# Selector products of k and q over 64 rows in a chunked delta-rule recurrence, both leaf parities issued in turn

## The reference

```python
def step(S, t):
    q_t, k_t, v_t, a_t, b_t = t
    y = jnp.einsum('bhvk,bhk->bhv', S, k_t)
    err = y - v_t
    S = a_t[..., None] * S - (b_t[..., None] * err)[..., None] * k_t[:, :, None, :]
    o = jnp.einsum('bhvk,bhk->bhv', S, q_t)
    return (S, o)
...
o = (o - mu) * jax.lax.rsqrt(var + LN_EPS) * ln_g + ln_b
g = jax.nn.sigmoid(x @ Wg).reshape(b, t, H, D)
o = (o * g).reshape(b, t, H * D)
return o @ Wo
```

## Time and profile before

| | us |
|---|---|
| median of 3 runs | 3279.95 (3260.17 to 3297.73) |
| the profiled execution: span | 3278.4 |
| stage of the recurrence in it (32 chunks) | about 630 to 2880 |
| PE busy | 2940.9 (90%) |
| DVE busy | 2404.1 (73%) |
| ACT busy | 1621.8 (49%) |
| POOL busy | 1308.9 (40%) |

### The profile page before, as it was taken

The page is one execution under the profiler, slowest core; times in us unless marked ns, Lnnn a source line. Parts: engine busy times, 40 slices in busy tenths (PEclk is TensorE's granted clock), DMA queues, the critical chain, the costliest instruction groups (busy, mean ns, idle before and its releaser), DMA issues. The chain is left out here.

```text
span 3278.4 us, 48421 instructions
## 1 busy us (share of the span) xinstructions
PE 2940.9 (90%) x14232; PEld 2043.1 (62%) x14232; DVE 2404.1 (73%) x4837; ACT 1621.8 (49%) x3516; POOL 1308.9 (40%) x1577
## 2 busy tenths in 40 slices
PE   7999999688889898898988989898898888879999
PEld 3555555466667666676666766677676667635554
DVE  6777777678887888878888788878888888632322
ACT  6666666445555555555555555545555555311110
POOL 3667677534344434344343443333444334300000
PEclk9999999889999999999999999999999999989999
DMA  3556556622122221232222322222322222030000
GB/s 135 228 214 239 231 204 239 185 46 39 39 53 55 50 44 39 43 65 51 43 40 41 66 50 43 39 41 48 59 54 39 41 40 41 15 107 20 7 7 7
DMA packets 443033, 249.60 MB, mean 76 GB/s; under 512 B 401488, under 2 KB 413488, under 8 KB 440624
## 3 DMA queue, kind: packets, MB, share of 16 engines
q1 hardware_dynamic: 442816, 246.90, 27.7%
HBM read 141.88 MB, written 104.99 MB: 75 GB/s over the span
## 5 line engine op out<-in xcount | busy, mean ns | idle before, releaser
L265 DVE SCALAR_TENSOR_TENSOR A_acc<-A_psY,A_w,A_acc 128x410 f32<-128x410 f32 (+1 forms) x720 | 419.2, 637 | 151.6 <-ACT A_acc L334 151.6
L832 POOL TENSOR_TENSOR B_WT<-B_WT,B_G 128x128 f32<-128x128 f32 (+2 forms) x224 | 190.9, 852 | 779.1 <-issue 448.1
L1136 ACT ACTIVATE B_WL<-B_psT 128x128 f32<-128x128 f32 (+2 forms) x480 | 150.3, 313 | 530.2 <-PE B_psT L1555 530.2
L405 PE MATMUL A_psY<-A_xT,A_w 128*128 128x413 f32 (+1 forms) x960 | 347.2, 510 | 9.1 <-PE A_psAG L411 7.7
L192 POOL TENSOR_TENSOR A_outs<-A_outs,A_acc 128x410 f32<-128x410 f32 (+1 forms) x240 | 229.7, 987 | 216.8 <-ACT A_outs L342 216.8
L405 PEld LDWEIGHTS A_psY<-A_xT,A_w 128*128 128x128 f32 x960 | 180.2, 189 | 165.5 <-issue 164.2
L1047 DVE TENSOR_TENSOR B_NC<-B_NC,B_psM 128x256 f32<-128x256 f32 x480 | 199.0, 414 | 114.8 <-PE B_psM L1582 95.7
L1050 DVE TENSOR_REDUCE B_W<-B_NC 128x64 f32<-128x320 f32 x512 | 248.7, 486 | 17.6
L1582 PE MATMUL B_psM<-B_BD,B_WL 128*128 128x128 f32 x1536 | 238.7, 297 | 9.2
L334 ACT ACTIVATE A_acc<-A_psY,A_w 128x410 f32<-128x410 f32 (+1 forms) x240 | 166.1, 692 | 162.9 <-PE A_psY L405 161.2
L1582 PEld LDWEIGHTS B_psM<-B_BD,B_WL 128*128 128x128 f32 x1536 | 197.2, 198 | 75.5 <-ACT B_WL L1136 74.7
(11 more groups left out here) (198 smaller groups left out, 7045.7 us busy)
## 6 DMA issues: line engine op xcount, KB each, us to landing
B_KQ<-scr SPq DMA_DIRECT2D x96, 512.0 KB, 6.6
scr<-A_outs SPq DMA_DIRECT2D x48, 615.0 KB, 3.5
scr<-A_outag SPq DMA_DIRECT2D x32, 615.0 KB, 5.2
scr<-A_outs SPq DMA_DIRECT2D x48, 409.0 KB, 2.5
A_xc<-nbeta SPq DMA_DIRECT2D x16, 1024.0 KB, 6.1
B_A<-scr SPq DMA_DIRECT2D x32, 512.0 KB, 4.9
B_C<-scr SPq DMA_DIRECT2D x32, 512.0 KB, 4.5
B_G<-scr SPq DMA_DIRECT2D x32, 512.0 KB, 4.6
```

The source lines that it names most:

```text
L265: nc.vector.scalar_tensor_tensor(a, y, w[:, s, col:col + 1], a, ALU.mult, ALU.add)\
L405: last = nc.tensor.matmul(psY[p][:, y0:y0 + HALO + t1 - t0], wp[:, p, kt, :], xT[:, kt, t0:t1 + HALO], start=kt == 0, stop=kt == KT - 1)
L832: tt(dst, dst, gr, ALU.mult).then_inc(wsc.sem, 1)
L1136: copy = lambda out, in_: nc.scalar.activation(out, in_, ACT.Copy)
```

## The change

The number of products and of their columns stays. Four things change.

1. "kk", "qk": each product contracts over the 64 rows of its leaf parity alone, and the products of the two parities are issued in turn (`row_scalars`). The two parities write into different banks, so a pair of neighbouring banks holds what one or two banks held before: "kk" keeps two banks for each half of the chunk; "qk" takes three pairs, (0, l), (1, l), (2, l), where it took five single banks. The rows of job 2 of leaf 2 move to leaf 3.
2. "update": the 16 products had 64 rows before; they were issued as four of rows 0 to 63, four of rows 64 to 127, and so on, and are now issued in turn, for two banks at a time (`updates`).
3. The readers take two banks at once. `y_terms` has three DVE operations per chunk (1024, 1024 and 512 numbers on each partition), one behind leaf 1 and two behind leaf 4; it had five of 512 behind leaves 1, 1, 3, 4 and 4. `row_pairs` and `pairs_copy` wait for both parities before they begin.
4. The ring is allotted when the program is built: a single job takes the bank that has been held longest, a pair the two neighbours of which the later one has been held longest.

```diff
-    jobs = {0: out and [("qk", 0), ("qk", 1)],
+    jobs = {0: out and [("qk", 0, 0), ("qk", 0, 1)],
             1: [("own", 1, 0), ("own", 1, 1)],
-            2: [("ktok", 0), ("gram", 1)] + (out and [("qk", 2)] or []),
-            3: out and [("qk", 3), ("qk", 4)],
+            2: [("ktok", 0), ("gram", 1)],
+            3: out and [("qk", 1, 0), ("qk", 1, 1), ("qk", 2, 0), ("qk", 2, 1)],
...
-OUT_ROWS = [((0, 0, 2),), ((1, 1, 2),), ((2, 2, 2),), ((3, 3, 1), (0, 2, 1)), ((1, 3, 1), (0, 3, 1))]
+OUT_ROWS = [((0, 0, 2), (1, 1, 2)), ((2, 2, 2), (3, 3, 1), (0, 2, 1)), ((1, 3, 1), (0, 3, 1))]
+KEY_ROWS = ((0, 1, 3), (1, 2, 2), (2, 3, 1))
...
+            if job[1] in ("kk", "qk"):
+                first = min(range(RING - 1), key=lambda b: max(held[b][0], held[b + 1][0]))
+                place_in(first, n)
+                place_in(first + 1, n + 1)
+            else:
+                place_in(min(range(RING), key=lambda b: held[b][0]), n)
...
-                wait(dve, nlc, i, 1)
-                ps = rows(take_bank(dve, g if h else g - 1, "kk", h, 0))
-                tt(n[:, :, :, :, 11], ps[:, 1], a[:, 1], ALU.mult).then_inc(nl.sem, 1)
-                tt(n[:, :, :, :, 16], ps[:, 2], rr, ALU.mult).then_inc(nl.sem, 1)
                 wait(dve, nlc, i, 2)
-                ps = rows(take_bank(dve, g if h else g - 1, "kk", h, 1))
-                tt(as_rows(X[:])[:, 1], ps[:, 1], a[:, 2], ALU.mult).then_inc(nl.sem, 1)
+                ps = take_two_banks(dve, g if h else g - 1, "kk", h)
...
-                wait(dve, awm, o, (4, 5, 3, 6, 6)[n])
-                ps = take_bank(dve, o + 1, "qk", n)
-                x = WX[:, 2 * n:2 * n + 2]
-                tt(x, ps[:].rearrange("p (n c) -> p n c", n=2), x, ALU.mult).then_inc(yv.sem, 1)
+                wait(dve, awm, o, (5, 6, 6)[n])
+                m = 4 if n < 2 else 2
+                ps = take_two_banks(dve, o + 1, "qk", n)[:, :, 0:m * HJ2]
+                x = WX[:, 4 * n:4 * n + m].rearrange("p k (l x) -> p l k x", l=2)
+                tt(x, ps.rearrange("p l (k x) -> p l k x", k=m), x, ALU.mult).then_inc(yv.sem, 1)
...
+            def row_scalars(g, kind, n):
...
+                filled = [open_bank(pe, g, kind, n, leaf)[1] for leaf in range(2)]
...
+                for k, (r, t0, m) in enumerate(runs):
+                    for leaf in range(2):
+                        p = slice(64 * leaf, 64 * leaf + 64)
+                        c = R * leaf + r
+                        last = mm(ps[:, leaf, at * width:(at + m) * width].rearrange("p (t x) -> p t x", t=m),
+                                  source[p, c:c + 1].to_broadcast([64, 128]),
+                                  rows[p, R * leaf + t0:R * leaf + t0 + m], start=True, stop=True)
...
+            def updates(g, half):
...
+                for m in range(4):
+                    i = 4 * half + m
+                    for r, (ps, filled) in enumerate(opened):
+                        p = slice(64 * r, 64 * r + 64)
+                        last = mm(ps[:, 128 * m:128 * (m + 1)], KTOK[p, i, :], WTOK[p, i, :], start=True, stop=True)
```

More of the change, by code:

```diff
@@ L445, in chunk_jobs @@
     if g == NCH:
[L446 removed]
+        return [("qk", n, l) for n in range(3) for l in range(2)] + [("oc", 0), ("oc", 1), ("var", 0), ("dev", 0), ("rstd", 0), ("rstd", 1)]
     if g > NCH:
@@ L540, in recurrence @@
         att = sb("att", [128, HID])
-        ring = [ctx.enter_context(nc.psum_tensor(f"B_ring{i}", [128, 512], FP32)) for i in range(RING)]
+        banks = ctx.enter_context(nc.psum_tensor("B_ring", [128, RING, 512], FP32))
+        ring = [banks[:, i] for i in range(RING)]
         psT = ctx.enter_context(nc.psum_tensor("B_psT", [128, 512], FP32))
@@ L615, in taken @@
             return {"contact": (cont, g, n + 1), "ktok": (ktok, g, n + 1), "decay": (stg, g, n + 1),
-                    "update": (stu, g, n + 1), "qk": (yv, g - 1, n + 1), "oc": (oc, g - 1, n + 1),
+                    "update": (stu, g, n + 1), "oc": (oc, g - 1, n + 1),
                     "var": (sd, g - 1, 1), "dev": (rd, g - 1, 1), "rstd": (on, g - 1, n + 1)}[kind],
         def open_bank(pe, *job):
-            n = JOBS.index(job)
-            if n >= RING:
-                for use in taken(*JOBS[n - RING]):
+            if before[job]:
+                for use in taken(*before[job]):
                     wait(pe, *use)
-            return ring[n % RING], full[n % RING]
+            return ring[place[job][0]], full[place[job][0]]
         def take_bank(eng, *job):
@@ L631, in take_bank, with two_banks, take_two_banks @@
             return ring[b]
+        def two_banks(*job):
+            b, _ = place[(*job, 0)]
+            return banks[:, b:b + 2]
+        def take_two_banks(eng, *job):
+            for leaf in range(2):
+                b, k = place[(*job, leaf)]
+                eng.wait_ge(full[b], k)
+            return two_banks(*job)
         FQ = SQ[:].rearrange("p h c -> p (h c)")
@@ L1127, in _ @@
                 chunk(g)
-            for n in range(5):
+            for n in range(3):
                 y_terms(NCH - 1, n)
@@ L1522, in shared_job @@
-                last.then_inc(filled, 1)
+                last.then_inc(filled, 1)
+            def row_scalars(g, kind, n):
+                if kind == "qk":
+                    rows, runs, width = QS[:, (g - 1) % 2].rearrange("p t h n -> p t (h n)"), OUT_ROWS[n], HJ2
+                else:
+                    rows, runs, width = KS[:], KEY_ROWS, HJ2 // 2
+                filled = [open_bank(pe, g, kind, n, leaf)[1] for leaf in range(2)]
+                if kind == "qk":
+                    wait(pe, qs, 2 * (g - 1) + 1, 1)
+                else:
+                    wait(pe, ks, 2 * g + (1 if n else 2), 1)
+                ps = two_banks(g, kind, n)
+                at = 0
+                for k, (r, t0, m) in enumerate(runs):
+                    for leaf in range(2):
+                        p = slice(64 * leaf, 64 * leaf + 64)
[3 more added lines that the diff above has]
+                                  rows[p, R * leaf + t0:R * leaf + t0 + m], start=True, stop=True)
+                        if k == len(runs) - 1:
+                            last.then_inc(filled[leaf], 1)
+                    at += m
@@ new lines, in updates @@
+            def updates(g, half):
+                opened = [open_bank(pe, g, "update", 2 * half + r) for r in range(2)]
+                wait(pe, wtok, g, half + 1)
+                wait(pe, ktok, g, 2)
+                for m in range(4):
[3 more added lines that the diff above has]
+                        last = mm(ps[:, 128 * m:128 * (m + 1)], KTOK[p, i, :], WTOK[p, i, :], start=True, stop=True)
+                        if m == 3:
+                            last.then_inc(filled, 1)
```

88 lines of the change are left out of this document (41 added, 47 removed).

## The result

The changed kernel takes 3300.35 us in the median (3294.4 to 3309.92, 20 runs) against 3282.08 us (3260.17 to 3297.73, 20 runs) for the kernel before: ratio 1.0057, 95% interval 1.0041 to 1.0073. It is slower by about 19 us, as forecast in sign and size (3294 us; range 3245 to 3325). The difference is small, but its interval leaves out 1.

The account below looks back on a forecast made before the run. No engine fills a chunk alone; the ring DVE, PE, ACT, PE bounds it. From 3278.4 us, 18.6 us gained at equal clock and 34.4 us lost to the clock gave 3294 us, range 3245 to 3325.

Parts of the forecast that it names:

- Which stages count: Whole chunk: shorter side jobs are worth something only at a few places; leaves 0 to 3 gain nothing.
- Rival 2: Whole chunk: TensorE's savings count; all of 158 us would give 3120 us, a third 3226 us; chance 0.15.
- The halves run side by side: kk, qk, updates: row halves overlap; 12 kk passes about 0.9 us, updates 1.92 us, about 5.1 us of PE's time a chunk.
- Rival 4: kk and updates: halves issued in turn don't run side by side; updates need 3.84 us, total 3300 us; chance 0.06.
- Leaf 4 to 6: Leaves 4 to 6: despite DVE's 1.81 us burst, earlier kk and leaf 5 transpose gain 0.38 us a chunk.
- Rival 3: Leaf 4: DVE's longer burst is not absorbed because kk waits longer for its bank; 3322 us; chance 0.17.
- Leaf 10 and 11, "nothing at full clock": Leaf 10's second kk: shortening it to 0.9 us only lengthens TensorE's wait from 0.76 to 1.6 us; no gain.
- The boundary: Chunk boundary: updates finish 0.87 us earlier, of which 0.22 us is gained (bounds: loss 0.1, gain 0.5).
- At equal clock: Whole chunk without clock effects: 0.60 us gained a chunk, over 31 chunks 18.6 us.
- The clock: From about 41 us into nearly every chunk: clock falls, 1.9 us each, 59 us less the present 25, 34 us lost.
- Rival 1: Whole kernel: the clock falls no more often than now, so only the 18.6 us gain counts; 3260 us; chance 0.20.

Follow-up runs that it names:

- e5: Changed kernel with y_terms cut 1024, 512, 1024 behind leaves 1, 3 and 4, products for the 512 back behind leaf 2: 3272.77 us, ratio 0.9985.
- e7: Changed kernel with e5's y_terms, 10 of var's 16 passes moved behind leaf 10's kk, and gram 5 of leaf 9 issued twice: 3229.83 us, ratio 0.9851.
- e9: The kernel of e7 with gram 0 of leaf 12 and decays 2 and 3 of leaf 13 also issued twice in even chunks: 3219.71 us, ratio 0.982.
- e11: Kernel before with gram 5 of leaf 9 issued twice, plus only the state's updates issued alternately: 3249.11 us, ratio 0.9903.
- e4: Changed kernel with its 64-row products (kk, qk, updates) issued one parity after the other: 3331.8 us, ratio 1.0152.
- filled kernels: Leaf 9's gram 5 issued twice: in the changed kernel, with leaf 10's kk also twice, 3251.54 us; in the kernel before, 3260.11 us.
- filled kernel before: Kernel before with gram 5 of leaf 9 issued twice: 3260.11 us, ratio 0.9942.

## Why the prediction was right, step by step

- **Which stages count: right.** Leaves 0 to 3 did not move, and TensorE's 86 us less bought nothing. Rival 2 (the savings count) is out by the 128-row "qk" too. One thing was missed there: the early fall of the clock at leaf 3, in chunks 19 and 23. The kernels with the third "qk" back behind leaf 2 (e5, e7, e9) have none.
- **The halves run side by side: right.** Twelve passes of "kk" in 0.99 us (predicted 0.9), the updates in 2.06 (predicted 1.92). Rival 4 is out: the rule that it was drawn from speaks of the order of starts and ends, not of passes one at a time. The term was 7 to 10% short, and the "kk" of leaf 10, mixed with the leaf's own products, takes 1.19 us. Over "qk", "kk" and updates TensorE saves 4.2 us a chunk instead of 5.1.
- **Leaf 4 to 6: right,** 0.37 us against 0.38, with the burst of 1.81 us as worked out and the transpose at 18.34 us (forecast 18.33). Rival 3's point of decision, "kk" more than 0.85 us late, was far off: it started 0.22 us later in its chunk (16.46 against 16.24).
- **Leaf 10 and 11, "nothing at full clock": wrong.** The prediction priced TensorE's wait alone and left out that `row_pairs` waits for both of ACT's copies here too, without a later idle time to absorb it: DVE comes 0.2 us later (2.34 us behind leaf 11's first step instead of 2.13), and once the clock is held it loses its turn before POOL, and the step costs 0.20 us. At leaf 5 it had named the same wait and found its cover.
- **The boundary: mis-sized,** 0.05 us for 0.22. From the updates' start to the next leaf 0 the change does gain 0.20 us (7.28 to 7.08). But the updates start 0.25 instead of 0.10 us after ACT's copy has ended (idle 0.45 instead of 0.30 us); the opening of a second bank now stands ahead of them. The same 0.45 us stand in e11, which has nothing of the change but the updates, and in e4, where the passes are issued in the old order; so it is the opening, and not the order of the passes. Without it the term would have been right.
- **At equal clock: 0.60 us a chunk predicted, about 0.2 found.** The sum of leaf 6, leaf 11 and the boundary is -0.37 + 0.20 - 0.05 = -0.22 us, 7 us in all instead of 18.6. The filled kernels, one of which pays 0.14 us a chunk for its doubled "kk", show 0.0 and 0.23 us without the step of leaf 8.
- **The clock: right.** 31 falls (forecast: nearly every chunk), 1.9 us each in even and 2.3 in odd chunks by the leaf steps, 1.73 by the filled kernel's span (predicted 1.9). The 14 falls of before cost 28 us by the lengths of their chunks (seven even ones 1.46 us over the undisturbed mean, seven odd ones 2.49; predicted 25); filling gave back 21.1 of them. In all 32.5 us by the spans against 34.4. Rival 1 is out. The error of the equal-clock sum, 12 us, is nearly the whole distance between 3294 and the 3304.2 of the trace; that the median, 3300, lies closer is the scatter of the runs.

## What to carry to other kernels

Before a side job of TensorE is made shorter, look at what fills the engine around it. Where other engines set the pace, the time saved turns into a wait, and if that wait lies in the thinnest stretch of a period it can cost the clock of the work behind it. Cut such a job only together with work moved into the gap; here 10 passes of useful work there, and a second issue of cheap products where none could be moved, together with y_terms back behind its old leaves, turned +0.6% into -1.8%. When a change regroups a reader's operations along with the products, measure it without the regrouping: here that gave away 0.46 of 0.85 us a chunk. When a reader is made to wait for two results instead of one, price it at each place where it runs: one had a gap to take it up, the other lost a race for a shared port.

## What the runs showed of the hardware

- Passes of 64 rows on different halves of the array overtake one another. In the rows of leaf 10 above, a "kk" pass starts at 1519.03 between two passes of L1617 (1519.01 and 1519.23), though it is issued behind both. L1617 is on rows 0 to 63; that this "kk" pass is one of rows 64 to 127 follows from the program, the trace does not name the half. The Trainium skill, "TensorE: Matmul & The Clock Gate", Part 3, has matmuls start strictly in program order; the starts in this trace do not. Issued in turn, 32 passes of 128 columns take 2.06 us, in groups of eight for one half 2.79; the contact's, over 128 rows, took 3.84.
- Issuing the same matmuls twice made this kernel 1.4% faster. A fall of the clock at leaves 10 to 13 cost 1.9 to 2.3 us in the changed kernel, and one of 13.7 us across a chunk boundary 5.4 us in the filled kernel before (71.3 us against 65.9).
- Where DVE and POOL want SBUF at nearly the same moment, a lead of 0.02 to 0.05 us decides which of the two is held, and here over 0.2 us on the critical path. The order was the same in 24 to 26 of 26 chunks of a filled kernel. At leaf 8 another near tie goes either way: the step is 0.46 us longer in 8 of 15 undisturbed chunks of the kernel before.
